# L1 attention of a ViT tower: three quarters of the exponentials and the gate at the head of the next pair, the backward values at the end of their own, new tile sequences

## The reference

```python
def _L1_attn_ref(x, wqv_w, wqv_b, wk, fanin_w, fanin_b):
    v = (x @ wqv_w.T + wqv_b).reshape(b, t, 3 * h, d)
    q, vf, vb = (v[:, :, :h], v[:, :, h:2 * h], v[:, :, 2 * h:])
    k = x[:, :, None, :] * wk[None, None]
    a = _l1_scores(q, k)        # -sum_w |q[s,h,w] - k[t,h,w]| / sqrt(w)
    a = concatenate([a, zeros], axis=1)
    a = softmax(a, axis=1)[:, :t]
    bf = einsum('bsdh,bshw->bdhw', a, vf)
    bb = einsum('bdsh,bshw->bdhw', a, vb)
    o = (bf + bb).sum(axis=2).reshape(b, t, d)
    y = o * sigmoid(1.702 * o)
    return x + y @ fanin_w.T + fanin_b
```

## Time and profile before

| | |
|---|---|
| median of 3 runs | 2394.49 us (2393.45 to 2395.8) |
| profiled execution, its own time | 2395.6 us |
| its span | 2393.8 us |
| busy: PE, DVE, ACT, POOL | 90%, 86%, 71%, 71% of the span |
| L1 attention stage | about 697 to 2300 us |
| chain that ended last, by engine | PE 41%, DVE 40%, issue 13%, ACT 3% |

### The profile page before, as it was taken

The page is one execution under the profiler, slowest core; times in us unless marked ns, Lnnn a source line. Parts: engine busy times, 40 slices in busy tenths (PEclk is TensorE's granted clock), DMA queues, the critical chain, the costliest instruction groups (busy, mean ns, idle before and its releaser), DMA issues.

```text
span 2393.8 us, 48808 instructions
## 1 busy us (share of the span) xinstructions
PE 2161.9 (90%) x13399; PEld 1001.3 (42%) x13399; DVE 2066.4 (86%) x2497; ACT 1691.6 (71%) x4540; POOL 1704.4 (71%) x969
## 2 busy tenths in 40 slices
PE   5475999999929999999999999999999999999978
PEld 4352333333303444444444444444444444444456
DVE  2877777777779999999999999999999999999963
ACT  1232434334318888888888888888888888888865
POOL 0111333333329999999999999999999999999933
PEclk9797999999959999999999999999999999999989
DMA  4301333332202222222222222222222222222201
GB/s 121 89 1 39 80 77 78 75 74 70 70 21 55 57 55 54 53 54 54 56 56 56 54 53 54 54 55 56 56 55 54 54 53 54 56 56 56 54 14 30
DMA packets 169426, 135.47 MB, mean 57 GB/s; under 512 B 45661, under 2 KB 151070, under 8 KB 169247
## 3 DMA queue, kind: packets, MB, share of 16 engines
q1 hardware_dynamic: 159850, 118.02, 20.0%
q10 hardware_dynamic: 9532, 16.91, 3.0%
HBM read 10.51 MB, written 4.19 MB: 6 GB/s over the span
## 4 chain that ended last, share of the span: by engine, by line
PE 41%; DVE 40%; issue 13%; ACT 3%; ACTq 1%; DMA 1%; DVEq 1%; POOL 0%; SPq 0%; POOLq 0%
DVE score L1569 29%; PE pp L854 9%; PE pp L842 4%; PE pp L791 3%; DVE absd L1509 3%; PE pp L760 3%; PE pp L661 2%; PE pp L753 2%; PE pp L786 2%; ACT absd L1082 1%; PE pp L686 1%; PE pp L953 1%; PE pp L846 1%; PE pp L682 1%; ACTq L1069 1%
## 5 line engine op out<-in xcount | busy, mean ns | idle before, releaser
L1569 DVE TENSOR_REDUCE score<-pp 128x16 f32<-128x1024 f32 x1280 | 1479.5, 1213 | 89.9 <-PE pp L854 89.5
L1685 POOL TENSOR_TENSOR absd<-absd 128x2560 f32<-128x2560 f32 x635 | 1445.4, 2276 | 80.6 <-ACT absd L1149 39.1
L854 PE MATMUL pp<-blocks,pick 128*128 128x512 f16 x2560 | 756.1, 382 | 40.8 <-DVE score L1569 25.9
L1149 ACT ACTIVATE absd<-pp 128x512 f32<-128x512 f32 x1280 | 696.3, 599 | 73.4 <-PE pp L842 54.1
L842 PE MATMUL pp<-blocks,pick 128*128 128x512 f16 x1280 | 393.5, 381 | 0.6 <-ACT absd L1149 0.5
L854 PEld LDWEIGHTS pp<-blocks,pick 128*128 128x128 f16 x2560 | 191.9, 97 | 429.7 <-DVE score L1569 340.2
L1652 POOL TENSOR_TENSOR absd<-absd,yw 128x512 f32<-128x512 f32 x112 | 142.3, 1271 | 307.3 <-DVE yw L1493 307.2
L1082 ACT ACTIVATE absd<-pp 128x512 f32<-128x512 f32 x256 | 149.5, 597 | 203.4 <-PE pp L683 156.2
L1509 DVE SCALAR_TENSOR_TENSOR absd<-pp,absd 128x512 f32<-128x512 f32 x256 | 171.5, 686 | 81.3 <-ACT absd L1082 68.4
L842 PEld LDWEIGHTS pp<-blocks,pick 128*128 128x128 f16 x1280 | 118.9, 97 | 190.5 <-ACT absd L1149 40.7
L1179 ACT ACTIVATE expd<-attn 128x65 f32<-128x65 f32 x512 | 156.4, 315 | 0.0
(11 more groups left out here) (229 smaller groups left out, 2660.8 us busy)
## 6 DMA issues: line engine op xcount, KB each, us to landing
blocks<-qk SPq DMA_DIRECT2D x1032, 64.0 KB, 2.0
blocks<-gT SPq DMA_DIRECT2D x128, 128.0 KB
blocks<-gT ACTq DMA_DIRECT2D x128, 128.0 KB
attn<-score SPq DMA_DIRECT2D x256, 64.0 KB, 2.1
xs<-xn SPq DMA_DIRECT2D x66, 32.0 KB, 1.8
big<-in_wrb_t SPq DMA_DIRECT2D x1, 2064.0 KB
big<-in_x_rows SPq DMA_DIRECT2D x4, 512.0 KB, 6.2
token_rows<-big SPq DMA_DIRECT2D x8, 256.0 KB, 2.0
```

What stands on the lines that cost most here:

```text
L854: mm = pe.matmul(ps[bank + n], pick[:, unit % 8 + n, :], blocks[:, b, unit // 16, unit // 8 % 2, :], start=True, stop=True)
L1149: nc.scalar.activation(absd[odd][:, 16 * u + 8 * n:16 * u + 8 * n + 8, :], ps[4 + n].rearrange("p (h w) -> p h w", w=D), ACT.Abs).then_inc ...
L1569: dve.tensor_reduce(score[:, odd, b, 16 * d:16 * d + 16], pp[:, bank:bank + 2, :].rearrange("p n (h w) -> p (n h) w", w=D), AX.X, ALU.add, ...
L1685: nc.gpsimd.tensor_tensor(x[:, :, 0:w], x[:, :, 0:w], x[:, :, w:2 * w], ALU.add).then_inc(X["tree"], 1)
```

## The change

The two sequences change. In both the fifth A unit stands at k = 11 and no longer at 12. On PE the backward values of a pair move from k = 1 of the next pair to the end of their own (behind E), the forward values from k = 3 to 2, turn and fan-in of y to k = 2 and 4 of the pair after; the three parts of attend stand at k = 10, 12 and 13 and no longer at 10, 10 and 11. On ACT parts 1 to 3 of the exponentials and the tanh move from the second image to the head of the next pair, part 0 stands one place later; the other copies follow PE. On DVE gated, finish and reciprocals move into the first image of the pair. Behind the loop stands what the moved work leaves over. Cut to its core:

```diff
-ORDERS = ("DADADDADDADDADED", "DADDADADDADDADDE")
+ORDERS = ("DADDADADADDADDED", "DADDADADDADADDDE")
...
                     if b == 0:
-                        if k == 1 and at >= 1:
-                            values_b(q - 1, 1 - odd, at)
-                        if k == 3 and at >= 1:
-                            values_f(q - 1, 1 - odd)
-                        if k == 4:
+                        if k == 2:
+                            if at >= 1:
+                                values_f(q - 1, 1 - odd)
+                            if at >= 3:
+                                turn_y(q - 3)
+                        if k == 4 and at >= 3:
+                            fan_in(q - 3)
+                        if k == 6:
                             turn(q + 1, at)
-                        if k == 7 and at >= 1:
+                        if k == 9 and at >= 1:
                             sum_e(q - 1, at == 1)
-                        if k == 10:
+                        if k == 12:
                             queries(q + 1, at)
-                        if k == 13 and at >= 1:
-                            turn_e(q - 1)
                         if k == 15:
+                            if at >= 1:
+                                turn_e(q - 1)
                             low(q + 1, 1 - odd, 0)
...
                             if k == 10:
                                 attend(q - 2, odd, 0)
+                            if k == 12:
                                 attend(q - 2, odd, 1)
-                            if k == 11:
+                            if k == 13:
                                 attend(q - 2, odd, 2)
-                            if k == 14:
-                                turn_y(q - 2)
-
-                if at >= 3:
-                    fan_in(q - 3)
+                        if k == 15:
+                            values_b(q, odd, at + 1)
...
             last = PAIRS - 1
-            values_b(last, 1, 4)
             values_f(last, 1)
+            turn_y(last - 2)
             fan_in(last - 2)
...
                 s, first = 2 * q, at == 0
+                if at >= 2:
+                    exponentials(q - 2, 1, at == 2)
+                if at >= 3:
+                    gate_o(q - 3)
                 absolute(s, 0, 0, q, first)
+                if at >= 2:
+                    exponentials(q - 2, 2, at == 2)
+                if at >= 3:
+                    turned_y(q - 3)
...
                 if at >= 1:
-                    for part in range(2):
-                        exponentials(q - 1, part, at == 1)
-                absolute(s, 1, 3, q, first)
-                if at >= 1:
-                    for part in range(2, 4):
-                        exponentials(q - 1, part, at == 1)
-                if at >= 2:
-                    gate_o(q - 2)
-                absolute(s, 1, 4, q, first)
-                if at >= 2:
-                    turned_y(q - 2)
+                    exponentials(q - 1, 0, at == 1)
                 absolute(s, 1, 5, q, first)
+                values_b(q, odd, at < 2)
...
             last = PAIRS - 1
-            values_b(last, 1, False)
+            for part in range(1, 4):
+                exponentials(last - 1, part, False)
+            gate_o(last - 2)
+            turned_y(last - 2)
             values_f(last, 1)
...
-                        if b == 0 and d == 0 and at >= 3:
-                            finish(q - 3, slot)
-                        if b == 1 and d == 7 and at >= 2:
-                            gated(q - 2)
-                        if b == 1 and d == 9 and at >= 1:
-                            reciprocals(q - 1)
+                        if b == 0:
+                            if d == 0 and at >= 3:
+                                gated(q - 3)
+                            if d == 2 and at >= 3:
+                                finish(q - 3, slot)
+                            if d == 5 and at >= 2:
+                                reciprocals(q - 2)
```

More of the change, by code:

```diff
@@ L1208, in pair @@
                 s, first = 2 * q, at == 0
+                if at >= 2:
+                    exponentials(q - 2, 1, at == 2)
+                if at >= 3:
+                    gate_o(q - 3)
                 absolute(s, 0, 0, q, first)
-                if at >= 1:
-                    values_b(q - 1, 1 - odd, at < 3)
-                absolute(s, 0, 1, q, first)
-                prepare_x(q + 1, 1 - odd)
+                if at >= 2:
+                    exponentials(q - 2, 2, at == 2)
+                if at >= 3:
+                    turned_y(q - 3)
+                absolute(s, 0, 1, q, first)
+                absolute(s, 0, 2, q, first)
+                prepare_x(q + 1, 1 - odd)
+                if at >= 1:
+                    values_f(q - 1, 1 - odd)
+                if at >= 2:
+                    exponentials(q - 2, 3, at == 2)
+                absolute(s, 0, 3, q, first)
+                if at >= 1:
+                    copy_e(q - 1)
+                absolute(s, 0, 4, q, first)
                 if at >= 2:
                     normalise(q - 2, 0, at == 2)
-                absolute(s, 0, 2, q, first)
-                if at >= 1:
-                    values_f(q - 1, 1 - odd)
-                    copy_e(q - 1)
-                absolute(s, 0, 3, q, first)
-                if at >= 2:
-                    normalise(q - 2, 1, at == 2)
-                absolute(s, 0, 4, q, first)
+                high_q(q + 1, False)
+                absolute(s, 0, 5, q, first)
                 if at >= 1:
                     take_e(q - 1, 1 - odd, at - 1)
-                high_q(q + 1, False)
-                absolute(s, 0, 5, q, first)
                 low(q + 1, 0)
@@ L1230, in pair @@
                 absolute(s, 1, 0, q, first)
+                if at >= 2:
+                    normalise(q - 2, 1, at == 2)
                 high_k(q + 1)
@@ L1236, in pair @@
                     turned_attn(q - 2)
+                absolute(s, 1, 3, q, first)
+                absolute(s, 1, 4, q, first)
                 if at >= 1:
-                    for part in range(2):
-                        exponentials(q - 1, part, at == 1)
-                absolute(s, 1, 3, q, first)
-                if at >= 1:
-                    for part in range(2, 4):
-                        exponentials(q - 1, part, at == 1)
-                if at >= 2:
-                    gate_o(q - 2)
-                absolute(s, 1, 4, q, first)
-                if at >= 2:
-                    turned_y(q - 2)
+                    exponentials(q - 1, 0, at == 1)
                 absolute(s, 1, 5, q, first)
+                values_b(q, odd, at < 2)
             act.wait_ge(pads, PADS)
@@ L1593, in _ @@
             last = PAIRS - 1
+            gated(last - 2)
+            reciprocals(last - 1)
             finish(last - 2, slice(last - 2, last - 1))
```

## The result

The change makes the kernel faster: 2379.57 us (median, 2375.16 to 2381.64) against 2394.01 for the kernel before in the same session, ratio 0.9936 with a 95% interval of 0.9919 to 0.9953. The prediction was 2378 with a range of 2373 to 2392. The profiled execution took 2381.58 us, its span is 2379.7, so 14.1 less than the 2393.8 of before.

What follows compares the result with a forecast made beforehand. The prediction took PE's dense stretch to bound the kernel before, and POOL the changed one (0.57). POOL's waits -15.3, lead -3.0 and tail +2.0 gave -16.3; 2395.6 - 16.3 - 1.1 = 2378 us, range 2373 to 2392.

Steps and rivals of the forecast that it cites:

- What bounds it before: L1 attention stage: PE sets the 24.58 us a pair; POOL's need lies 0.25 below it, DVE's 1.4.
- PE's dense stretch: PE without gaps from 1512.66 to 1521.64: attends, turn of y, fan-in, both values, six D units; sets the period.
- POOL's waits go, -15.3: POOL's waits after the stage's first, 15.3 us in 61 pairs, would vanish, leaving its need of 24.33 us a pair.
- The free period of 24.15: Time in which PE, ACT and DVE could turn a pair: 23.2 us plus about 0.97 idle.
- The walk: One pair of the new order stepped through with durations from the old trace, giving some 24.15 us.
- half the gain: Rival, chance 0.22: latencies together 0.25 us more, period 24.40, no lead, tail +2, so 2385.5 us.
- The lead of 3.0: Loop's end: the last E can come 3.0 us before POOL's last batch ends, where it came with it: -3.0.
- The tail of +2.0: Behind the loop: from E to the taken column some 8.5 us instead of 6.5, so +2.0.
- A units: no wait of their own: Fifth A unit from k 12 to k 11: POOL's batches ready 12.85 and 11.3 us apart, costing no wait.
- The ring of y: Chain of tanh, gated, turn, copy of y, fan-in, finish on ACT, DVE, PE: tanh 0.3 us to spare, copy none.
- the slower rival: Rival, chance 0.09: ACT reaches tanh or the copy of y 0.60 us later, period 24.75, so 2407 us.
- POOL's idle time: Of POOL's 1.2 idle us a pair only 0.25 counted as open; the skill's occupancy rule would open all, some 71 us.

Runs made afterwards that it cites:

- the lighter tree: The last addition (128x160) of POOL's tree left out: 2394.55 us in the kernel before, 2359.78 us in the changed kernel.
- the heavier one: POOL's addition of 128x160 done twice in each batch: 2439.62 us in the kernel before, 2445.17 us in the changed kernel.
- the new sequences alone: The kernel before with only the two new sequences (fifth A unit at k = 11): 2495.36 us.
- one attend block ahead of E: The reordered tail version, with backward values moved behind k 13 of the second image and the third attend block behind k 14: 2399.33 us.
- the reordered tail: The version with joint steps, with ACT's work behind the loop in another order and DVE's finish ahead of the reciprocals: 2360.85 us.
- the version with joint steps: The changed kernel with the last two steps of POOL's tree done once for both images of a pair: 2360.46 us.
- the exponentials put back: The changed kernel with all four parts of the exponentials in the second image of their own pair, as before: 2384.20 us.

## Why the prediction was right

- **What bounds it before.** Right that POOL doesn't: the lighter tree changed nothing, and the heavier one hid 0.22 of its 1.06 a pair in POOL's waits. That it is PE's dense stretch rests on DVE's waits and on what moving blocks did; PE wasn't made lighter or heavier in any run.
- **POOL's waits go, -15.3.** Right: 0.2 is left of them (and 1.2 of "issue" is new), and POOL ended 15.0 earlier. POOL's need is 24.36 instead of 24.33.
- **The free period of 24.15.** It is 24.01. The walk had 0.61 + 0.14 around the end of the pair (by its own starts the 0.14 is 0.10), 0.05 and 0.17 elsewhere; the runs with a light POOL show 0.51 at the first reduction and nothing else that is listed. So the walk charged small crossings that cost nothing listed. The error had no price, because POOL's need lay above both values; that part of the hit is luck. With 24.01 the bound is POOL more clearly than I had given it (0.57), and "half the gain" was further off.
- **The lead of 3.0.** 2.06. The walk took E 21.3 us after the first abs of a pair. But ACT waits for POOL in the second image, not at the pair's first abs as the prediction said. From that wait's end (1496.94) E comes 10.0 later (1506.95) and the end of POOL's next batch 12.05 later (1508.99), which leaves the 2.0. The sign was right, and that the lead comes of a freed buffer; the place was wrong.
- **The tail of +2.0.** +3.3, the term most off. PE's clock, which the sum hadn't in it, is 1.5 of that (below), a little more than the miss. Reordered, the tail was 2.7 shorter in a trace.
- **A units: no wait of their own.** Right for POOL: the fifth A unit's absolute values are there 3.6 us before POOL takes them. But I had taken the sequence for a matter of A units, as the expectation of the new sequences alone says openly. It isn't: with the blocks at numbered places it decides what stands between two D units, and alone it costs 101 us. The prediction didn't pay for this, because its walk moved both together.
- **The ring of y** had its 0.3 to spare on the tanh: DVE's `gated` isn't among the waits of the changed kernel. The copy of y had nothing to spare, as the walk said: PE's weight load for fan-in waits 0.18 a pair for it (9.4 us in 52), just under the 0.2 that would have spoken against the prediction, and no listed wait of DVE follows. A late ring is real, though: one attend block ahead of E brought it about, at 24.65 us, where the slower rival had said 24.75 with the delay coming from a part of the exponentials.
- **POOL's idle time.** Of 1.2 us a pair only the waits went; POOL is busy 239.99 of 250 us where the kernel is wholly bound by it. The Trainium skill's measure of occupancy (Perfetto Trace Analysis, Identifying the Most-Contended Engine) would still show 10 us open there. No run here got any of that back by order; the one that got some had fewer instructions.

Sum: -15.0 - 2.1 + 3.3 = -13.8 (13.9 unrounded) against -16.3. The misses of 0.3, 0.9 and 1.3 all point the same way. The time is nearer than the terms: 2379.57 against 2378, while the four runs lie 6.5 us apart. The mechanism is shown by the runs, the closeness of the number is partly chance.

## What to carry to other kernels

Before working on waits, make each engine that could be the next bound a little lighter or heavier in a run of its own: here one addition less on POOL said in two runs that the old kernel doesn't gain by it and the new one does, and how much. Read a hand-written schedule by the time from one unit that feeds the engine in question to the next, here against 1.14 us of reduction, and treat sequence and places as one object. What passes unnoticed beyond the 1.14 isn't a constant: it is how far the engine is behind at that place, 0.43 in one and 0.08 in others, where units or blocks before had used it up. When an order has made one engine the bound, count its small instructions: joining two of 0.45 and 0.32 us cost a few lines and gave 19 us on top of the reordering's 14. Without the new order a lighter POOL gave nothing.

## What the chip showed unasked

The clock granted to PE falls behind the last pair in every trace looked at, but in the longer tail it fell early enough to stretch work that the end waits for. Windows of the changed kernel behind the last pair (PE, PEld, DVE, ACT, POOL, clock):

```profile
2262.00:2266.00 4.00, 2.40 (x15) 0.95 (x12) 1.39 (x3) 3.59 (x16) 2.43 (x5) 1.00 0.00 0
2266.00:2269.00 3.00, 2.16 (x15) 1.30 (x19) 1.65 (x4) 0.74 (x2) 0.40 (x1) 0.63 0.17 46
2269.00:2272.00 3.00, 1.85 (x12) 0.93 (x4) 3.00 (x1) 0.96 (x5) 0.00 (x0) 0.50 0.00 0
```

It went from 1.00 (2.4 GHz) to 0.50 (1.2 GHz) just ahead of fan-in (a window from 2266.50 to 2267.00 gives 0.78), after PE had stood idle 0.68 for the backward values' copy and 1.09 in the row that hangs on the tanh. Fan-in then took 0.69 us, the column sum 1.96 and the turn of the column 1.04. Before, with the clock at 1.00, they took less, and the clock fell only after them:

```profile
2282.28 0.43 PE L801 MATMUL pp<-fan,yT 96*128 96x64 f32 x2
2283.03 1.09 PE L814 MATMUL pp<-absd,pair_ones 128*32 128x256 f32 x16 [0.32 <-DVE h L1564]
2284.64 0.62 PE L821 MATMUL pp<-row_of,esum 128*128 128x16 f32 x4 [0.52 <-ACT esum L1159]
...
2285.00:2288.00 3.00, 0.77 (x6) 0.70 (x6) 3.00 (x1) 2.10 (x9) 0.00 (x0) 0.94 0.08 22
```

The version with the reordered tail has the same three lengths (0.43, 1.09, 0.62), at a clock of

```profile
2243.00:2246.00 3.00, 1.85 (x22) 1.01 (x20) 1.86 (x3) 1.99 (x12) 0.00 (x0) 1.00 0.09 25
```

So 0.26 + 0.87 + 0.42, some 1.5, of the tail's +3.3 is the clock, and a delay that only seems to shift PE's work also stretches it.

POOL's additions don't scale down: 128x320 takes 0.72 to 0.86 us, 128x160 0.45 to 0.47, 128x80 0.32, so halving the size from 160 saves 0.13 of 0.45. And the runs of one kernel scatter differently from version to version: the changed kernel's four lie 6.5 us apart, the version with joint steps has 0.6. It doesn't go by the bound: with POOL as the bound the exponentials put back have 1.5, with PE, ACT and DVE as the bound the reordered tail has 5.3. The cause stays open.
